# Two flat cross attentions: scores as 64 keys by two heads in four banks, exponentials over two banks, maxima pieces one bank at a time, values padded with zeros

## What is computed

```python
q = x @ Wq; k = ctx @ Wk; v = ctx @ Wv            # 1024 queries, 6404 keys
scores = einsum('bhqd,bhkd->bhqk', q, k) * 8 ** -0.5
scores = where(masked, -inf, scores)
probs = softmax(scores, axis=-1)
out = einsum('bhqk,bhkd->bhqd', probs, v) @ Wo
```

## Time and profile before

| | |
|---|---|
| median of 3 runs | 6178.66 us (6174.67 to 6187.05) |
| profiled execution, span | 6180.5 us, 82959 instructions |
| PE busy | 4319.4 us (70%) |
| DVE busy | 3667.5 us (59%) |
| ACT busy | 2628.5 us (43%) |
| POOL busy | 756.9 us (12%) |
| masked `cross`, from its first piece to its last exponential | 1556 to 3084 us |
| unmasked `cross`, the same | 3379 to 4526 us |

### The profile page before, as it was taken

The page is one execution under the profiler, slowest core; times in us unless marked ns, Lnnn a source line. Parts: engine busy times, 40 slices in busy tenths (PEclk is TensorE's granted clock), DMA queues, the critical chain, the costliest instruction groups (busy, mean ns, idle before and its releaser), DMA issues. The chain is left out here.

```text
span 6180.5 us, 82959 instructions
## 1 busy us (share of the span) xinstructions
PE 4319.4 (70%) x31970; PEld 1559.0 (25%) x31970; DVE 3667.5 (59%) x7693; ACT 2628.5 (43%) x4771; POOL 756.9 (12%) x842
## 2 busy tenths in 40 slices
PE   5956999544699999999964899999877641134224
PEld 2333444333122222222242122222134320012011
DVE  5464666556877777777345998998724650137122
ACT  2522666224366666666611587888730110001001
POOL 0000000002000000000002000000000027722772
PEclk9878999767799999999976899999988875567567
DMA  0020000024000000000004001100014000000000
GB/s 13 1 62 10 15 11 9 15 100 155 18 12 10 3 12 12 12 12 1 1 6 104 1 12 19 17 12 12 1 15 147 13 5 13 12 5 5 13 13 8
DMA packets 119874, 141.87 MB, mean 23 GB/s; under 512 B 48269, under 2 KB 96620, under 8 KB 116846
## 3 DMA queue, kind: packets, MB, share of 16 engines
q1 hardware_dynamic: 77870, 118.15, 7.6%
q0 software_dynamic: 20480, 10.53, 1.1%
q10 hardware_dynamic: 21128, 7.88, 0.5%
HBM read 103.35 MB, written 33.14 MB: 22 GB/s over the span
## 5 line engine op out<-in xcount | busy, mean ns | idle before, releaser
L1480 ACT ACTIVATE probs<-ps 128x512 f32<-128x512 f32 x3264 | 1734.3, 598 | 763.0 <-PE ps L1425 762.9
L1515 DVE CUSTOM_DVE_ANT_0 junk<-ps,mask 128x512 bf16<-128x512 f32 (+1 forms) x1664 | 1049.1, 678 | 362.5 <-PE ps L1387 346.4
L1510 DVE TENSOR_REDUCE maxima<-ps 128x2 f32<-128x1024 f32 (+1 forms) x832 | 956.2, 1199 | 110.6 <-PE ps L1387 104.2
L1441 PE MATMUL ps<-probs,vstack 128*9 128x512 f32 x6528 | 873.0, 596 | 0.4 <-ACT probs L1480 0.4
L1425 PE MATMUL ps<-qturned,kturned 52*128 52x512 bf16 x3264 | 792.8, 385 | 83.7 <-ACT probs L1480 64.8
L1387 PE MATMUL ps<-kturned,qturned 49*128 49x512 bf16 (+1 forms) x3328 | 704.6, 392 | 110.8 <-DVE maxima L1510 35.7
L3172 POOL DMA_INDIRECT line<-table,index x640 | 644.8, 1008 | 876.9 <-DVE index L3545 483.5
L1418 PE MATMUL ps<-maskT,lower 128*128 128x512 fp8e5 x1632 | 562.3, 387 | 63.5 <-ACT probs L1480 15.1
L1425 PEld LDWEIGHTS ps<-qturned,kturned 52*128 52x128 bf16 x3264 | 196.2, 93 | 791.8 <-ACT probs L1480 462.1
L1387 PEld LDWEIGHTS ps<-kturned,qturned 49*128 49x128 bf16 x3328 | 166.3, 95 | 492.7 <-DVE maxima L1510 200.3
L1418 PEld LDWEIGHTS ps<-maskT,lower 128*128 128x128 bf16 x1632 | 123.5, 96 | 598.6 <-ACT probs L1480 433.4
(11 more groups left out here) (718 smaller groups left out, 4826.6 us busy)
## 6 DMA issues: line engine op xcount, KB each, us to landing
raw<-in_mask_BxSxS_if SPq DMA_DIRECT2D x8, 3202.0 KB, 13.2
kturned<-keys_parts SPq DMA_DIRECT2D x192, 102.0 KB
table<-lines SPq DMA_DIRECT2D x51, 256.0 KB, 3.0
line<-table,index POOLq DMA_INDIRECT x640
keys_parts<-parts SPq DMA_DIRECT2D x24, 384.0 KB, 2.7
vstack<-values_heads SPq DMA_DIRECT2D x16, 459.0 KB, 16.5
lose<-in_mask_SxS_bc SPq DMA_DIRECT2D x32, 128.0 KB
values_heads<-vall SPq DMA_DIRECT2D x2, 1728.0 KB, 10.4
```

What stands on the lines that cost most here:

```text
L1441: last = nc.tensor.matmul(k.ps[at:at + HD + 1, 3, :], vstack[:, p % 2, a, t, :], probs[:, (h * KT + t) % slots, a, :], start=(t < 2), stop ...
L1480: nc.scalar.activation(probs[:, u % slots, a, :], k.ps[:, (2 * u + a) % 3, :], ACT.Exp, scale=(1.0 if maskT is None else 1.0 / STEP8)).the ...
L1510: nc.vector.tensor_reduce(dst, ring(e).rearrange("p (a n) -> p a n", a=2)[:, :, 0:hi - lo], AX.X, ALU.max).then_inc(ring_free[at % 2], 1)
L1515: nc.vector.tensor_tensor_reduce(junk[:, at % 2, a * BANK:a * BANK + hi - lo], ring(e)[:, a * BANK:a * BANK + hi - lo], mask8[:, 4 * b + m ...
```

## The change

- **Scores.** One step makes both heads of a unit. The 128 keys are cut in two groups of 64 (`first`), and four matmuls of 64 keys each go to two banks: head `a` of group `first` to partitions `64 * (a ^ first)` on, of bank `bank + first`. Units take two pairs of banks in turn, so scores hold four banks. One exponential covers 1024 columns. The mask matmul takes `split`, made in the setup, for one group of 64 keys twice over.
- **Pieces.** One piece is one head: 104 per half, each in one bank of a ring of three. The masked and the unmasked attention both take the fused subtract and maximum; the unmasked one subtracts a tile of zeros.
- **Values.** A value matmul gives 18 rows for both heads, with zeros where the keys belong to the other head. `vall` and `values_heads` double in size, POOL clears the zero strips in `context_sides`, DVE copies the values in two instructions per group, and `vstack` is loaded with four DMAs for a pair of heads, where it was one.
- **Order.** `programme` puts one half of a unit's pieces ahead of the weigh and one behind it.

```diff
-LEAD = 3
+LEAD = 6
+RING = 3
+PAIR = 2 * (HD + 1)
-    return [(m, c) for m in range(4) for c in range(len(CHUNKS))]
+    return [(m, c, a) for m in range(4) for c in range(len(CHUNKS)) for a in range(2)]
...
-            cut = [-(-len(spread) * (3 * t + j) // (3 * KT)) for j in range(4)]
-            if masked:
-                out += [("score", h, t, 0), ("score", h, t, 1)] + spread[cut[0]:cut[2]]
-            else:
-                out += [("score", h, t, 0)] + spread[cut[0]:cut[1]] + [("score", h, t, 1)] + spread[cut[1]:cut[2]]
-            out += late.pop(h * KT + t, []) + spread[cut[2]:cut[3]]
+            cut = [-(-len(spread) * (2 * t + j) // (2 * KT)) for j in range(3)]
+            out += [("score", h, t)] + spread[cut[0]:cut[1]] + late.pop(h * KT + t, []) + spread[cut[1]:cut[2]]
...
             def score(e):
-                _, h, t, a = e
+                _, h, t = e
...
+                if u >= 2:
+                    pe.wait_ge(probs_ready, u - 1)
+                if maskT is not None:
+                    for first in range(2):
+                        nc.tensor.matmul(k.ps[:, bank + first, :], k.split[:, first, :], maskT[:, t, mine],
                                          start=True, stop=False, skip_group_check=True)
...
+                for first in range(2):
+                    for a in range(2):
+                        rows = slice(a * SLOT, a * SLOT + ROWS)
+                        to = slice(64 * (a ^ first), 64 * (a ^ first) + 64)
+                        last = nc.tensor.matmul(k.ps[to, bank + first, :], kturned[rows, par, t * P + 64 * first:t * P + 64 * first + 64],
+                                                qturned[rows, par, mine], start=maskT is None, stop=True, skip_group_check=True)
+                last.then_inc(scores_filled, 1)
...
-                    nc.scalar.activation(probs[:, u % slots, a, :], k.ps[:, (2 * u + a) % 3, :], ACT.Exp,
+                    nc.scalar.activation(probs[:, u % slots].rearrange("p b n -> p (b n)"),
+                                         k.ps[:, bank:bank + 2, :].rearrange("p b n -> p (b n)"), ACT.Exp,
...
-                if maskT is None:
-                    dst = maxima[:, b, :, c].rearrange("p (a m) -> p a m", a=2)[:, :, m]
-                    nc.vector.tensor_reduce(dst, ring(e).rearrange("p (a n) -> p a n", a=2)[:, :, 0:hi - lo], AX.X,
-                                            ALU.max).then_inc(ring_free[at % 2], 1)
...
+                lost = nothing[:, 0:hi - lo] if mask8 is None else mask8[:, 4 * b + m, lo:hi].bitcast(mybir.dt.uint8)
+                nc.vector.tensor_tensor_reduce(junk[:, at % RING, 0:hi - lo], ring(e)[:, 0:hi - lo], lost, 1.0, -3.0e38,
+                                               ALU.subtract, ALU.max, maxima[:, b, 4 * a + m, c:c + 1]).then_inc(ring_free[at % RING], 1)
...
+                if g < 4:
+                    for a in range(2):
+                        nc.gpsimd.memset(vall[:, 2 * g:2 * g + 2, a, :, 1 - a, :], 0.0).then_inc(strips_cleared, 1)
```

More of the change, by code:

```diff
@@ L167, in _ @@
             nc.vector.tensor_scalar(k.lower[:], k.ident[:], LOWER, None, ALU.mult).then_inc(zeroed, 1)
+            for first in range(2):
+                for half in range(2):
+                    nc.vector.tensor_scalar(k.split[:, first, 64 * half:64 * half + 64], k.ident[:, 64 * first:64 * first + 64],
+                                            LOWER, None, ALU.mult).then_inc(zeroed, 1)
             if n_bf:
@@ L1266, in cross @@
     slots = 6 if maskT is not None else 8
-    steps = programme(3, maskT is not None)
-    ring_at, ring_clear, ring_read = {}, {}, {}
-    frees = [0, 0]
+    steps = programme(3)
+    ring_at, last_piece = {}, {}
     for e in steps:
         if e[0] in ("piece", "queries", "shifted", "sums"):
-            at = len(ring_at) % 2
             ring_at[e] = len(ring_at)
-            ring_clear[e] = frees[at]
-            frees[at] += 2 if e[0] == "piece" and maskT is not None else 1
-            ring_read[e] = frees[at]
+            if e[0] == "piece":
+                last_piece[e[1], ring_at[e] % RING] = e
     with Stage(nc) as s:
@@ L1300, in cross @@
         ring_filled = s.sem("ring_filled")
-        ring_free = [s.sem(f"ring_free{i}") for i in range(2)]
+        ring_free = [s.sem(f"ring_free{i}") for i in range(RING)]
         dve_order = s.sem("dve_order")
@@ L1339, in _ @@
                                      k.ends_dram.unsqueeze(0)).then_inc(ends_loaded[par], 16)
-                sp.dma_start(vstack[:, par].rearrange("p a t d -> p (a t d)"),
-                             k.values_dram[:, 2 * p:2 * p + 2].rearrange("p a t d -> p (a t d)")).then_inc(values_loaded[par], 16)
+                for first in range(2):
+                    keys = slice(64 * first, 64 * first + 64)
+                    for a in range(2):
+                        rows = slice(64 * (a ^ first), 64 * (a ^ first) + 64)
+                        sp.dma_start(vstack[rows, par, first].rearrange("p t d -> p (t d)"),
+                                     k.values_dram[keys, 2 * p + a].rearrange("p t d -> p (t d)")).then_inc(values_loaded[par], 16)
         @block.gpsimd
@@ L1384, in piece @@
                 lo, hi = CHUNKS[c]
-                for a in range(2):
-                    rows = slice(a * SLOT, a * SLOT + SHIFT)
-                    last = nc.tensor.matmul(ring(e)[:, a * BANK:a * BANK + hi - lo], qturned[rows, par, t * P:(t + 1) * P],
-                                            kturned[rows, par, lo:hi], start=True, stop=True)
-                last.then_inc(ring_filled, 1)
+                rows = slice(a * SLOT, a * SLOT + SHIFT)
+                nc.tensor.matmul(ring(e)[:, 0:hi - lo], qturned[rows, par, t * P:(t + 1) * P], kturned[rows, par, lo:hi],
+                                 start=True, stop=True).then_inc(ring_filled, 1)
             def queries(e):
@@ L1451, in add_up @@
                 for m in range(4):
-                    last = nc.tensor.matmul(ring(e)[:, m * 32:m * 32 + 2 * (HD + 1)], sums[:, h % 2, m * P:(m + 1) * P], fold[:],
+                    last = nc.tensor.matmul(ring(e)[:, m * 32:m * 32 + PAIR], sums[:, h % 2, m * P:(m + 1) * P], fold[:],
                                             start=True, stop=True)
                 last.then_inc(ring_filled, 1)
-            pe.wait_ge(cleared, 4)
+            pe.wait_ge(cleared, 5)
             for e in steps:
@@ L1503, in piece @@
                 b = h % 2
-                m, c = half[i]
+                m, c, a = half[i]
                 lo, hi = CHUNKS[c]
```

124 lines of the change are left out of this document (61 added, 63 removed).

## The result

The changed kernel takes 6511.65 us in the median of four runs (6437.39 to 6586.28), the one before 6182.85 us on the same chip (6174.67 to 6190.68). The ratio is 1.0454, with a 95% interval of 1.0407 to 1.0500. The forecast was 6277 us. The direction was right; the size lies outside the range.

A forecast was written before the change was run, and what follows sets the result against it. PE was taken to bound the masked middle and DVE, with PE close behind, the unmasked one. Terms of +77 + 10 + 5 - 27 + 34 = +99 us on the profiled 6180.5 us gave 6277 us, range 6140 to 6350.

The forecast's parts named there:

- unmasked middle: Unmasked attention's 15 halves with pieces: PE 1014 us, DVE 984, taken as 1025 us; +10 us, from -31 to +40.
- Masked window: Masked attention: middle pair from 3.45 to 3.65 us, +77 us; tail pair from 3.23 to 2.68 us.
- the second mask's wait of 0.32 us: Masked middle: PE's wait per pair for a bank ACT has not emptied; four score banks were to end it.
- The price of the shape change: PE between 52*64 scores and 49*128 pieces: 0.1 us added, scores to piece 0.33 us; 0 as other end.
- the lone piece: Masked middle: the second piece behind the weigh has no partner to run beside and costs a full 0.31 us.
- Tail, unmasked: Unmasked attention's last 51 units, without pieces: pair from 2.37 to 1.83 us, -0.54 over 25 pairs.
- Head: Unmasked attention's opening pieces: 52 x (1.22 - 1.13), +5 us; nothing in the masked one.
- Making keys and values: `context_sides`: POOL's memsets, 1.77 us each, DVE's half copies and the stores; +34 us, from +15 to +55.
- The three stores: Stores of keys and values, doubled in bytes: 0 to 10 us for a store, 5 taken per attention.
- Rival 1: Score steps: four scores take two rounds, both heads writing one bank, 0.21 us per step; 6604 us, chance 0.15.
- Rival 2: Both middles: the change of tile width costs nothing; masked -8, unmasked -25 us; 6158 us, chance 0.20.
- Rival 3: No change in effect: width change half price in masked stage, keys and values +15; near 6200 us, chance 0.08.

The follow-up runs named there:

- e1: Changed kernel with scores again two 128-key matmuls, one head per bank, 9-column values and the old `context_sides`; 5927.89 us, ratio to before 0.9965.
- e6: e1 with an 18-column weigh: its own nine columns and those of the next key tile; 5931.27 us, ratio to before 0.9965.
- e9: e1 with unmasked score matmuls ordered so the first takes the array half of the piece ahead of it; 5921.14 us, ratio to before 0.9953.
- e0: The changed kernel itself, run again beside the others; 6273.39 us, ratio to before 1.0494.
- e5: Changed kernel with a weigh of 9 columns instead of 18, leaving out the second head's values; 6223.09 us, ratio to before 1.0480.
- e2: Changed kernel with all of a unit's pieces ahead of its weigh; 6133.06 us, ratio to before 1.0316.
- e4: Changed kernel with the edits of e1 and e2 together; 5996.70 us, ratio to before 1.0088.
- e3: Changed kernel with one useless 128*128 matmul of 512 columns ahead of each unmasked unit's scores; 6333.60 us, ratio to before 1.0651.
- e8: Changed kernel with four idle matmuls ahead of the first scores of each unmasked half; 6216.03 us, ratio to before 1.0448.
- e10: e8 plus one idle matmul in each of the first 16 units of the unmasked stage; 6145.44 us, ratio to before 1.0278.

## Why the prediction was right and wrong

**The step that failed** is in the unmasked middle: "PE and DVE, at 1014 and 984, then both stand where the stretch of 1015.5 us is now." It took over the clock of 1.00 in the earlier trace rows for a stage whose matmuls had changed, and no rival had the clock as its place. The granted clock was 0.85, and of the 210.6 us some 160 are that. Without them the profiled execution would have taken about 6325 us, inside the range and still slower than before: an estimate, from 6484.9 - 160.

The cause, as far as the runs separate it, is the scores' shape of 52*64 in a loop with pieces on both sides of the weigh and no 128*128 matmul in it. In this order wide scores keep the clock (e1, e6, e9: at most 18 us low), and narrow ones lose it whatever the weigh's width (changed, e0, e5). With the pieces together the shape matters little (137.2 us low in e2, 117.8 in e4). Narrow scores with a 128*128 matmul beside them keep it: the masked attention, which has its mask matmuls, at 1.00, and e3 with its filler. The fall comes where PE waits at an edge or at a fold; e8 and e10 remove those at the edges. But before and e1 wait at the edges too (0.52 and 1.28 us) and no low spell of theirs lasts over 10 us, where the changed kernel stays down for up to 156 us, and in e0 238. What differs most is how long the clock takes to come back. The Trainium skill (TensorE: Matmul & The Clock Gate, Part 1: The HAM clock gate) describes a clock that follows how busy the engine has lately been. By busy time alone this trace disagrees: PE is busy 50.00 of 50 us at 3830 and stays at 1.2 GHz.

**At full clock** the terms came out as follows.

- Masked window: +77 and a tail of -14 were forecast, +63; +74.7 measured. Pair 3.65, measured 3.70; the second mask's wait of 0.32 us is gone, as said. In the tail ACT's pair is 2.74 us, forecast 2.68:

```profile
3140.73 1.94 ACT L1494 ACTIVATE probs<-ps 128x1024 f32<-128x1024 f32 x2 [0.80 <-PE ps L1438]
3143.47 1.94 ACT L1494 ACTIVATE probs<-ps 128x1024 f32<-128x1024 f32 x2 [0.80 <-PE ps L1438]
```

- The price of the shape change, 0.1 us, and the lone piece are confirmed by taking them away: e1 shortens the masked window by 96.3 us (0.25 us a pair for two score steps), e2 by 85.5.
- Unmasked middle: forecast +10. A half without a low spell takes 72.3 us (the first scores behind the edges stand at 3605.4, 3677.4 and 3750.1), where before takes 67.9 (13 halves from 3510.9 to 4393.2): 4.4 x 15 = +66 us. The pair is 2.62 us (4100.23 to 4102.85), not 2.57, which makes 1.3 us of a half, and an edge takes 5.5 us beyond its 25.5 pairs where the sum had 2.1. So this term too lies beyond its upper end of +40. With the tail's -12 below, full clock accounts for 54 of the 210.6 us; the rest, 157, stands beside the 155 to 172 that the low spells make at 0.40 to 0.44.
- Tail, unmasked: 39 exponentials in 36.98 us, a pair in 1.90, forecast 1.83, where it took 2.37; 25 pairs give -12. Head: 68.5 us from its first piece to the first scores, where it took 63.6, so +5 as forecast.
- Making keys and values: forecast +34, measured +17 (51.8 to 60.0 us from the first memset to the turned mask in the masked attention, and 53.6 to 62.7 from it to the load of `fold` in the unmasked one). The memset was mis-sized. The row of 1.57 us in the earlier trace rows is POOL's first instruction for a long time; the new ones take half of what was worked out from it, two of 918 elements in 1.77 us:

```profile
1446.96 1.33 POOL L1178 TENSOR_TENSOR rest<-rest,parts 128x512 f32<-128x512 f32 x1
1448.36 0.61 POOL L1180 CAST parts<-rest 128x512 bf16<-128x512 f32 x1
1448.91 1.77 POOL L1176 MEMSET vall<- 128x918 f32 x2
```

- The three stores, twice as large, landed in 13.6, 10.7 and 13.4 us, where they took 10.4, 9.9 and 11.1; doubling cost 0.8 to 3.2 us each, as bounded.

**Rival 1** did not happen: 0.34 us from scores to piece, not 0.54. The rule of the Trainium skill behind it (TensorEngine Tiling (Array Packing), Gotcha 1: PSUM Pressure) does not cost time here, with two row tiles of different columns in one bank. **Rival 2** did not happen either; the change of width cost its 0.1 us. **Rival 3** had the change of width at half price, and it cost the whole; its lower end for keys and values, +15, is near the +17 measured.

**What stays open.** Why the narrow matmuls hold the clock down for so long was shown only by comparison of shapes; a loop of them without weighs was not tried. Whether e3's filler keeps the clock by its shape of 128*128 or only as more work for PE is not separated: a narrow filler was not tried. Each run with wide scores (e1, e6, e9) also drops the zeros between the values and loads `vstack` with one DMA in place of four; e3 has both and keeps its clock, but no run has narrow scores without them. And what decides at which edge or fold a fall comes, and for how long, is open, since both differ from one execution to the next.

## What to carry to other kernels

A clock of 1.00 in a stage belongs to its present mix of matmuls: where a change makes the weights narrower in a loop that fills PE, the lower clock is a rival with its own price (here 0.40 to 0.44 us lost for each us spent at 1.2 GHz), and the first thing to read afterwards is the granted clock by windows. Splitting a matmul into tiles that run abreast saved nothing here, and each change of weight shape cost about 0.1 us; whole 128-key scores with the same four banks and wide exponentials kept the gain of this change and left out its cost. An order of steps that is best in a stage bound by PE (pieces together) can be the worst in one bound by DVE, where a ring of three cannot carry it.

## What had not been expected of the hardware

PE stayed at 1.2 GHz for 156 us in the changed kernel and 238 us in e0, with its matmuls back to back, and came back to 2.4 GHz without any change in the program. In both executions the falls stood only where PE had stopped for up to 1.05 us, at an edge or behind a fold, and most such stops brought none. And the same program differed by 230 us between the first result and e0 in stages that the change does not touch (1660.3 and 1427.3 us behind the attentions), while its masked attention, at full clock, differed by 0.9 us. In the first result POOL waits 194 us for DVE's `prod` among its indirect gathers, and in the kernel before, taken with it, 195 us; e0 has no such wait. Why is not known.
